# An audio tower on one core: scores in a three-buffer PSUM ring of their own, all other jobs in two single banks, v times W0 per token tile

## What is computed

```python
h = _L0_tok_ref(x, ...)    # signs of x and kernel, width-3 convolution, batch norm: (4, 748, 64)
h = h + _L0_attn_ref(_layernorm(h), Wqkv, bqkv, W0, b0)
h = h + _L0_ffn_ref(_layernorm(h), w1s, b1s, w2s, b2s)

# attention, 8 heads of 64
q, k, v = jnp.reshape(x @ Wqkv + bqkv, (3, b, n, d, h))
score = jnp.einsum('bnqh,btqh->bnth', q, k) * d ** (-0.5)
attn = jax.nn.softmax(score, axis=1)
av = jnp.einsum('bnnh,bnqh->bnqh', attn, v)      # only the diagonal of attn is used
out = av.reshape(b, n, d * h) @ W0 + b0
# feed-forward: a binary tree of 255 nodes; each token follows one path of 8 nodes,
# out = sum over the path of gelu(|logit|) * (x @ w2s[node] + b2s[node])
```

## Time and profile before

| | |
|---|---|
| median of 3 runs | 580.06 us |
| profiled execution | 581.13 us, span 579.4 us |
| TensorE matmul busy | 403.5 us, 70% |
| VectorE busy | 372.9 us, 64% |
| ScalarE busy | 277.9 us, 48% |
| GpSimd busy | 307.8 us, 53% |
| mean granted TensorE clock | 0.849 |

### The profile page before, as it was taken

One profiled execution on the slowest core, in us unless ns is written; L12 is line 12 of the kernel. 1 busy time (PEld: TensorE's weight loads), 2 busy tenths in 40 slices (PEclk: granted clock), 3 DMA queues, 4 the chain that ended last, 5 costly groups with the idle time before them and its releaser, 6 DMA issues.

```text
span 579.4 us, 8416 instructions
## 1 busy us (share of the span) xinstructions
PE 403.5 (70%) x2782; PEld 286.3 (49%) x2782; DVE 372.9 (64%) x605; ACT 277.9 (48%) x615; POOL 307.8 (53%) x354
## 2 busy tenths in 40 slices
PE   1335688887987898888858898622314999287781
PEld 1224566565655565556645665411213777154550
DVE  0756757668677667774678586872982999733431
ACT  1344578768667866776637577410201010044541
POOL 2665308563355177843456771398746677752211
PEclk9977789989889987988869789955555999689997
DMA  4251404319969123212303120084004110200000
GB/s 115 70 120 47 115 13 107 92 42 215 193 127 158 36 67 79 59 37 66 81 0 80 37 72 1 7 124 75 12 12 126 31 41 24 76 9 4 5 6 10
DMA packets 57822, 37.53 MB, mean 65 GB/s; under 512 B 30846, under 2 KB 56429, under 8 KB 57772
## 3 DMA queue, kind: packets, MB, share of 16 engines
q1 hardware_dynamic: 54030, 33.96, 26.7%
q0 software_dynamic: 2944, 2.45, 1.5%
q10 hardware_dynamic: 800, 0.49, 0.3%
HBM read 11.33 MB, written 9.56 MB: 36 GB/s over the span
## 4 chain that ended last, share of the span: by engine, by line
PE 41%; DVE 24%; ACT 16%; issue 8%; POOL 7%; DMA 3%; ACTq 0%; SPq 0%; DVEq 0%; POOLq 0%
PE Z L834 11%; ACT Z L1099 7%; PE Z L963 4%; PE Z L790 4%; DVE lm L1456 4%; PE Z L746 4%; PE Z L737 4%; PE Z L792 3%; DVE nm L1258 3%; DVE va L1449 3%; ACT k L1043 3%; ACT q L1043 2%; PE Z L965 2%; DVE va L1284 2%; PE Z L815 2%
## 5 line engine op out<-in xcount | busy, mean ns | idle before, releaser
L1258 DVE TENSOR_REDUCE nm<-Z 125x1 f32<-125x748 f32 x192 | 172.8, 931 | 94.4 <-PE Z L834 91.8
L1099 ACT ACTIVATE Z<-Z,nm 125x748 f32<-125x748 f32 x192 | 164.9, 860 | 74.8 <-DVE nm L1258 74.6
L834 PE MATMUL Z<-pool_a 128*125 128x512 f16 (+1 forms) x768 | 162.7, 357 | 18.9 <-ACT Z L1099 12.6
L834 PEld LDWEIGHTS Z<-pool_a 128*125 128x125 f16 x768 | 98.6, 151 | 62.3 <-ACT Z L1099 20.9
L667 POOL DMA_INDIRECT out<-lm,va x44 | 43.1, 979 | 59.4 <-DVE lm L1462 52.7
L545 POOL TENSOR_TENSOR pool_a<-q,pool_a 128x748 f16<-128x748 f32 x16 | 26.2, 1635 | 60.4 <-DVE pool_a L1221 60.3
L1456 DVE TENSOR_REDUCE lm<-va 128x64 f32<-128x512 f32 x44 | 45.2, 1027 | 1.3
L790 PE MATMUL Z<-va,xhT 128*125 128x128 f16 x192 | 33.1, 257 | 17.4 <-ACT Z L1099 17.4
L1178 ACT COPY va<-Z 32x512 f32<-32x512 f32 x48 | 27.5, 573 | 34.5 <-PE Z L969 34.5
L1099 ACT ACTIVATION_READ_ACCUMULATOR Z<-Z,nm 125x1 f32 x192 | 39.5, 206 | 0.0
L737 PE MATMUL Z<-xhT,wq 128*128 128x249 f16 (+2 forms) x256 | 33.1, 278 | 8.7 <-ACT Z L1099 7.6
(11 more groups left out here) (208 smaller groups left out, 690.1 us busy)
## 6 DMA issues: line engine op xcount, KB each, us to landing
pool_a<-pool_a SPq DMA_DIRECT2D x64, 187.0 KB, 3.3
pool_a<-pool_a SPq DMA_DIRECT2D x64, 93.5 KB, 2.2
sorted_rows<-zrow SPq DMA_DIRECT2D x1, 3864.0 KB, 22.7
va<-sorted_rows SPq DMA_DIRECT2D x11, 276.0 KB, 5.4
w<-in_L_ffn_w2s SPq DMA_DIRECT2D x1, 2048.0 KB
lm<-in_x SPq DMA_DIRECT2D x4, 375.0 KB
pool_a<-in_L_ffn_w2s SPq DMA_DIRECT2D x1, 1024.0 KB
out<-lm,va POOLq DMA_INDIRECT x44, 2.2
```

The source lines that it names most:

```text
L834: last = mm(z[0:XP, c0:c1], kst[:, u % 3, a, hd, KST[t]:KST[t] + XP], qst[:, u % 3, hd, c0:c1], start=(a == 0), stop=(a == 1))
L1099: sc_.activation(z, z, ACT.Exp, bias=nm[0:XP, u % 4, i:i + 1], accum_out=sm[0:XP, u % 4, i:i + 1]).then_inc(s_fa, 1)
L1258: v.tensor_reduce(nm[0:XP, u % 4, i:i + 1], zone(("s", u, i))[0:XP, 0:N], X, ALU.max, negate=True).then_inc(s_max, 1)
```

## The change

1. **PSUM.** Scores alone go round three double buffers, `Z[n % 3]`, and wait for the exponentials three steps before. All other jobs go round two single banks, `E`, the halves of `Z[3]`, and wait for the job two before. Jobs are cut to fit 512 columns: q and k in two parts each, the transposes and ranks in two, the logits in three, the diagonal in three pieces behind three steps.
2. **v times W0.** For batches 0 to 2 a job is now one token tile for all eight heads (`yt`, three matmuls of 512 columns), six a batch, in the first two units after it (`ph` 0 and 1). `weigh_heads` handles 512 columns; `add_heads` halves them by three additions on GpSimd and adds the result to h. Batch 3 keeps pairs of heads (`yp`), in two parts.
3. **Tree.** GpSimd's `path_masks` goes from `ph` 3 to the next batch's `ph` 0, `leaf_masks` from 0 to 1, the layer norm from 1 to 2, `own_slots` from 0 to 3; TensorE's transposes and logits from `ph` 2 to 3 (last batch 2 to 1), ranks from 3 to 2.
4. **First stage.** x of batch 1 waits for batch 0, ScalarE's half of Wqkv is issued later; the low parts of the weights and of the first q and k go from GpSimd to VectorE (`first_lo`); `xh 1` and `normalise(2)` go behind the first scores.

```diff
-        FIRST = [("q", 0), ("k", 0), ("q", 1), ("k", 1), ("xb", 2), ("xb", 3), ("xh", 1), ("cv", 2)]
+        LASTB = NU - NPAIR
+        FIRST = [("xb", 2), ("xb", 3), ("cv", 2)]
...
             f = []
-            if 1 <= u <= NU and i == 0:
-                f.append(("d", u - 1))
-            if u + AHEAD < NU and i in (1, 3):
-                f.append(("qk"[i // 2], u + AHEAD))
-            f += {(0, 4): [("xh", 2)], (0, 5): [("cv", 3)], (0, 7): [("wt", 0)], (0, 9): [("wm", 0)],
-                  (0, 11): [("wt", 1)], (1, 2): [("wm", 1)], (1, 4): [("xh", 3)], (1, 5): [("wt", 2)],
-                  (1, 7): [("wm", 2)], (1, 9): [("cb", 0)], (1, 11): [("w1", 0)], (2, 5): [("y", 0)],
-                  (2, 9): [("y", 1)]}.get((u, i), [])
-            if 3 <= u <= NU and i == 5:
-                f.append(("y", u - 1))
-            if b >= 0 and ph == 2:
-                f += {5: [("t", b)], 8: [("l", b, 0)], 10: [("l", b, 1)]}.get(i, [])
-            if b >= 1 and (ph == 3 if b < B - 1 else ph == 1) and i == 7:
-                f.append(("r", b - 1))
-            if b == B - 1 and ph == 3 and i == 11:
-                f.append(("r", b))
+            if 1 <= u <= NU and i < 3:
+                f.append(("d", u - 1, i))
+            if u + AHEAD < NU and 3 <= i <= 6:
+                f.append(("q" if i < 5 else "k", u + AHEAD, 2 - i % 2))
+            f += {(0, 1): [("xh", 1)], (0, 2): [("wt", 0)], (0, 7): [("wm", 0)], (0, 8): [("xh", 2)], (0, 9): [("cv", 3)],
+                  (0, 11): [("wt", 1)], (1, 7): [("wm", 1)], (1, 8): [("xh", 3)], (1, 9): [("wt", 2)],
+                  (1, 11): [("wm", 2)], (2, 7): [("cb", 0)], (2, 9): [("w1", 0)]}.get((u, i), [])
+            if 0 <= b < B - 1 and ph < 2 and i in (7, 9, 11):
+                f.append(("yt", b, 3 * ph + (i - 7) // 2))
+            if u == NU - 2 and i in (7, 8, 10, 11):
+                f.append(("yp", LASTB + i // 10, (0, 1)[i in (8, 11)]))
+            if NU - 1 <= u <= NU and i in (7, 9):
+                f.append(("yp", u - 1, (i - 7) // 2))
+            if 0 <= b < B - 1 and ph == 3:
+                f += {7: [("t", b, 0)], 8: [("t", b, 1)], 9: [("l", b, 0)], 10: [("l", b, 1)], 11: [("l", b, 2)]}.get(i, [])
+            if 1 <= b and ph == 2 and i in (7, 9):
+                f.append(("r", b - 1, (i - 7) // 2))
+            if b == B - 1 and ph == 1:
+                f += {7: [("t", b, 0)], 8: [("t", b, 1)], 9: [("l", b, 0)], 10: [("l", b, 1)], 11: [("l", b, 2)]}.get(i, [])
+            if b == B - 1 and ph == 3 and i in (7, 9):
+                f.append(("r", b, (i - 7) // 2))
...
         def zone(f):
-            return Z[(number[f] + 3) % 4]
+            return E[number[f] % 2]
...
             load_x(0)
+            sp.wait_ge(s_xin[0], 16)
             load_x(1)
...
-            def w_lo(g):
...
             x_lo(0)
-            w_lo(1)
+            rstd1(1)
...
+            def add_heads(b, t):
+                k = NT * b + t
+                pool.wait_ge(s_wyv, k + 1)
+                if t == 0:
                     pool.wait_ge(s_hb, b + 1)
-                hv = xrow[0:XP, b * NT:(b + 1) * NT, C_H:C_ID]
-                pw = prod[0:XP, w % 2]
+                hv = xrow[0:XP, k, C_H:C_ID]
+                pw = prod[0:XP, k % 2, 0:8 * D]
+                for n in (4 * D, 2 * D, D):
+                    link(gp.tensor_tensor(pw[:, 0:n], pw[:, 0:n], pw[:, n:2 * n], ALU.add))
+                gp.tensor_tensor(hv, hv, pw[:, 0:D], ALU.add).then_inc(s_hy, 1)
+
...
-            part_lo("q", 0)
-            part_lo("k", 0)
             part_lo("q", 1)
             part_lo("k", 1)
-            rstd1(1)
...
                     token_numbers()
-                if u == 2:
+                if u == 3:
                     h_bias(0)
                     h_bias(1)
                     h_bias(2)
                     h_bias(3)
-                    add_heads(0)
-                    add_heads(1)
-                if 3 <= u < NU:
-                    add_heads(u - 1)
-                if 0 <= b < B - 1 and ph == 3:
-                    path_masks(b, pool, gp, link)
-                if 1 <= b and ph == 0:
-                    leaf_masks(b - 1, pool, gp, link)
-                if b >= 2 and ph == 0:
-                    own_slots(b - 2)
-                if 0 <= b < B - 1 and ph == 1:
+                if 0 <= b < B - 1 and ph < 2:
+                    for t in range(3 * ph, 3 * ph + 3):
+                        add_heads(b, t)
+                if u == NU - 2:
+                    add_pair(LASTB)
+                if NU - 2 <= u < NU:
+                    add_pair(u - 1)
+                if 0 <= b < B - 1 and ph == 2:
                     ln2_squares(b)
                     ln2_rstd(b)
                     ln2_x(b)
-                if b == B - 1 and ph == 1:
-                    ln2_rstd(b)
+                if 1 <= b and ph == 0:
+                    path_masks(b - 1, pool, gp, link)
+                if 1 <= b and ph == 1:
+                    leaf_masks(b - 1, pool, gp, link)
+                if b >= 2 and ph == 3:
+                    own_slots(b - 2)
+                if u == NU:
+                    ln2_rstd(B - 1)
                     pool.sem_inc(s_rs2, 1)
-            pool.wait_ge(*full(("s", NU - 1, 2 * NT - 1)))
+            pool.wait_ge(s_score, 2 * NT * NU)
             link(gp.memset(wlow[D:P, :], 0.0))
...
             def take(f):
-                if number[f] >= 4:
-                    pe.wait_ge(*freed[order[number[f] - 4]])
+                if number[f] >= 2:
+                    pe.wait_ge(*freed[order[number[f] - 2]])
...
+            def heads_out(b, t):
...
+                r0, g = v_tile(b, t)
+                for a in range(2):
+                    mm(z[0:XP, :], xhT[:, r0:r0 + XP], mw[:, a, g * H * D:(g + 1) * H * D], start=(a == 0), stop=False)
+                mm(z[0:XP, :], pick[:, g, 0:XP], cb[:], start=False, stop=True).then_inc(s_full, 1)
...
             def scores(u, i):
                 hd, t = divmod(i, NT)
-                z = take(("s", u, i))
+                n = 2 * NT * u + i
+                z = Z[n % 3]
+                if n >= 3:
+                    pe.wait_ge(s_exp, n - 2)
+                else:
+                    pe.wait_ge(s_first, n + 2)
...
+            def first_lo(kind):
+                n = "qk".index(kind)
+                dve.wait_ge((s_qc, s_kc)[n], 1)
+                v.tensor_tensor(hl[:, 0, n, 1, 0:N], (q32, k32)[n][:, 0, 0:N], hl[:, 0, n, 0, 0:N],
+                                ALU.subtract).then_inc(s_lo, 1)
...
             center(1, Z[1][:, 512:1024])
+            hi_cast("q", 0)
+            first_lo("q")
+            hi_cast("k", 0)
+            first_lo("k")
+            normalise(1)
             signs(2)
             signs(3)
-            hi_cast("q", 0)
-            hi_cast("k", 0)
             hi_cast("q", 1)
             hi_cast("k", 1)
-            normalise(1)
             center(2, zone(("cv", 2)))
-            normalise(2)
...
+            def weigh_heads(b, t):
+
+                k = NT * b + t
+                dve.wait_ge(s_at, NPAIR * (b + 1))
+                dve.wait_ge(*full(("yt", b, t)))
+                if k >= 2:
+                    dve.wait_ge(s_hy, k - 1)
+                w0 = NPAIR * b % 8
+                av = at[0:XP, w0:w0 + NPAIR, :].rearrange("p j (a t) -> p t j a", a=2)[:, t].unsqueeze(3).to_broadcast(
+                    [XP, NPAIR, 2, D])
+                v.tensor_tensor(prod[0:XP, k % 2, 0:8 * D].rearrange("p (j a o) -> p j a o", j=NPAIR, a=2),
+                                zone(("yt", b, t))[0:XP].rearrange("p (j a o) -> p j a o", j=NPAIR, a=2),
+                                av, ALU.mult).then_inc(s_wyv, 1)
+                dve.wait_ge(s_wyv, k + 1)
+                dve.sem_inc(s_fd, 1)
...
                         take(f)
-                    if (u, i) == (1, 1):
-                        normalise(3)
-                    if (u, i) == (1, 11):
+                    if (u, i) in ((0, 2), (1, 3)):
+                        normalise(2 + u)
+                    if (u, i) == (2, 9):
                         dve.wait_ge(s_ch, 1)
                         v.tensor_tensor(c32[:, 1, :], c32[:, 0, :], cb[0:3, :], ALU.subtract).then_inc(s_cl, 1)
-                    if 1 <= u <= NU and i == 4:
+                    if 1 <= u <= NU and i == 5:
                         diag_weights(u - 1)
-                    if u + AHEAD < NU and i in (3, 5):
-                        hi_cast("qk"[i // 4], u + AHEAD)
-                    if u == NU and i == 6:
+                    if u + AHEAD < NU and i in (6, 9):
+                        hi_cast("qk"[i // 9], u + AHEAD)
+                    if 0 <= b < B - 1 and ph == 2 and i == 2:
+                        ln2_sums(b)
+                    if 0 <= b < B - 1 and ph == 3 and i == 0:
+                        ln2_sumsq(b)
+                    if u == NU and i == 10:
                         last_heads(NU - 1)
```

(8 more changed lines are left out.)

284 lines of the change are left out of this document (150 added, 134 removed).

## The result

The changed kernel takes 584.66 us (median of 20 runs, 580.88 to 587.65); the kernel before took 583.49 in the 20 runs beside it. The ratio is 1.008, 95% interval [1.005, 1.011]: 0.8% slower, within the 2% that the prediction calls no change, but not the 570 us of the prediction. It is taken without the slow executions, over 1.5% above the fastest of their kernel, of which the kernel before had 8 and the changed kernel none; that is why it is larger than the 0.2% between the two medians. The profiled execution took 582.8 us, its span is 581.1 us at a clock of 0.823 (before: 579.4 and 0.849).

What follows compares the result with a forecast made beforehand. No engine was full in attention; engines waited for each other through the ring of four, where every other job takes a turn. 579.4 - 10 - 13 + 12 = 568.4 us of span, plus 1.7 around it: 570, range 548 to 592.

Steps and rivals of the forecast that it cites:

- the first stage: Up to the first maximum: batch 2's normalising goes behind the scores, low parts leave GpSimd; -10 us, from 3.7 to 13.
- attention: First maximum to last exponential: 315.5 us against 328.6, so -13, bounds -24 and +15.
- the tail: Behind the last exponential: GpSimd has more left and its memset may hold VectorE; +12 us, bounds +6 and +16.
- batch 2: Units 12 to 15: same wait for masks, y product parts and a wait for squares on top; 86.5 us against 82.1.
- the 6 us set apart for the clock: Over the four attention stretches: allowance for plain units at a granted clock of 0.75, 2.7 us longer each; 6 us.
- Prices of single operations: Product of 512 columns 0.70 us, a tile's additions 1.9, GpSimd's list from the cast of k to leaf masks 37.4.
- Batches 0 and 1: Units 4 to 7: 70 us against 75.7; units 8 to 11: 81 against 86.0, about 10 lost ahead of ranks.
- the last term, 19 us for unit 15: Last unit of batch 2, in the sum 52 + 15.5 + 19 = 86.5 us.
- The third: Gain drowns in GpSimd: additions take 3 us a tile or casts meet GpSimd instructions; +17, 587 us; chance 0.10.
- The second: TensorE's clock: more units at a mean clock of 0.75, attention stretches below 0.80; 594 us; chance 0.13.
- The first: Shorter units show in full: no clock loss, attention 306.5 us, first stage gives 12; 553 us; chance 0.27.
- the rule: GpSimd and VectorE's shared port pair is locked for the whole instruction; end +14 us by it, +6 without.

Runs made afterwards that it cites:

- the last kernel: Against the combined kernel: triple product buffer, VectorE's sums over h at step 8 instead of 2, ranks of batch 0 at steps 10 and 11; 550.0 us, 0.947.
- the new unit 14: Changed kernel with unit 14's y products at steps 3, 4, 7, 8 and ranks at 10, 11: 572.5 us; with sum of squares at step 3 too: 569.7.
- The run with the slots ahead of the memset: Changed kernel with the slots of batch B-2 issued on GpSimd just ahead of the large memset instead of behind it; 580.6 us, ratio 0.999.
- the combined kernel: Changed kernel with the new unit 14, sum of squares at step 3, x at once, slots of batches 0 and 1 in unit 15; 562.6 us, 0.967.
- the one with the triple buffer: Changed kernel with only the buffer of the products v times W0 made triple, so GpSimd may lag two tiles; 583.5 us, ratio 1.002.
- The last two kernels: The combined kernel with triple product buffer and sums at step 8: 557.8 us, 0.964; then also ranks of batch 0 at steps 10 and 11: 550.0, 0.947.

## Why the prediction was wrong

The forecast missed the profiled span by 12.7 us (568.4 against 581.1), and the sum shows where: +5.3 in the first stage, +10.0 in attention, -2.6 in the tail. In attention batch 2 is off by 11.4 us and the other three stretches by 4.7 together, less the 6 us set apart for the clock.

- **Prices of single operations: right.** The product of 512 columns took 0.68 us (0.70), a tile's additions 1.99 (1.9), the list to the leaf masks 38.2 (37.4). TensorE had the masks 50.6 us behind the first exponential of batch 1 (51) and 50.8 behind that of batch 2 (326.2 less 275.4; 52).
- **Batches 0 and 1: right**, 72.5 and 81.5 us against 70 and 81, although the 6 us for the clock were kept apart there. But the reason given for batch 1, "All scores stand behind it: about 10 us are lost" ahead of the ranks, was only part: TensorE waited 1.55 us there, since the waits for products and sums had held it up already.
- **Batch 2: the step that failed, in its last unit.** Up to the end of unit 14 the forecast has 52 + 15.5 = 67.5 us, and units 12 to 14 took 67.5; the wait for the squares is in it at 4 and was 4.22. What failed is the last term, 19 us for unit 15: it took 29.4. The four parts of y products were priced in unit 14 only. Unit 15 has two more, and its clock was put at nothing there. By the terms that the forecast names (12.5 + 3 + 17 + 4) the sum would also be 2 us larger than the 15.5 + 19 that it carries.

The last five steps of a unit with transposes and logits, from the exponential of step 7: unit 11 of the changed kernel, unit 15 of it, and unit 15 of the last kernel, with the same jobs on TensorE as the second (the counts differ by what else falls into the window):

```profile
268.10:275.40 7.30, 6.39 (x39) 4.96 (x37) 4.93 (x6) 6.66 (x16) 4.15 (x3) 1.00 0.53 126
357.50:372.20 14.70, 11.60 (x44) 8.48 (x42) 4.67 (x6) 6.64 (x15) 4.85 (x5) 0.64 0.04 12
```

```profile
337.30:348.30 11.00, 7.90 (x50) 6.17 (x48) 4.76 (x7) 6.62 (x15) 6.79 (x8) 1.00 0.11 34
```

At a clock of 1.00 the two y parts, which take turns in the two banks with the transposes and logits, cost 3.7 us; in both kernels TensorE waits 1.68 and 1.42 us there for a bank that VectorE empties. The same jobs at 0.64 take 3.7 more. With the 3.8 us by which the first seven steps are longer than those of unit 11, mostly the wait for the squares, that gives 29.4 from the 18.2 of unit 11. No run moves the two y parts of unit 15, so their price is read from these rows and not from an experiment. The 10.7 us that the new unit 14 took back are no miss of the forecast: they are waits that it had priced, and that another order avoids.

- **First stage: mis-sized.** I let the normalising of batch 2 go behind the scores and counted -10; it gave -4.7. The centring of batch 2 stayed ahead, with three operations at 1.47 to 2.07 us beside GpSimd (0.56 alone), and x of batch 1 came 2 us later. With both put right the first exponential stood at 41.6 us instead of 47.7. Besides, the term is not worth its size: the 3.2 us that the centring won at the first exponential came back in unit 0.
- **Tail: right**, +9.4 of +12 with bounds of +6 and +16, and VectorE's step was held. The run with the slots ahead of the memset shows what moving it is worth, 3.8 us, with another step then held for 3.49.
- **Rivals.** The third, at 587, came nearest in time, not in mechanism: the additions took what they should, and no cast of q or k took more than 0.80 us. The second spoke of a clock under 0.80; that came in batch 2 alone (0.77), and rose to 0.84 there (274.3 to 361.5 us of that run) when the jobs were reordered. So it holds in part, in batch 2, where unit 15 alone shows 3.7 us of it. The first is refuted as a forecast, but the last kernel, at 550.0, shows that the gain was there.

## What to carry to other kernels

When a slow engine's list has several readers, find all of them before moving one: each looks cheap in the trace (1.5 us for the masks, 1.3 for the sums), because the one in front hides the next, and the whole only shows when the last is moved. When a ring is made smaller, price a job not only by its length but by when its bank is emptied, in every unit that has the job, and look at what is queued on the emptying engine between. A wait of the critical engine costs nothing by itself while the engine behind it is still busy. Where a step is to be hidden in idle time of the critical engine's neighbour, check that the start that it wins isn't paid for in the next unit.

## What was not expected of the hardware

**Which VectorE steps a memset on GpSimd holds.** In the combined kernel the memset began before the ranks, and reductions ran beside it at their usual length (0.95 us for 768 columns); only the TENSOR_SCALAR was held to its end:

```profile
381.84 8.73 POOL L670 MEMSET pool_a<- 64x10368 f32 x1 [0.15 <-POOL run L338]
...
386.78 0.95 DVE L1387 TENSOR_REDUCE rank<-gt 128x6 f32<-128x768 f32 x1
...
389.84 0.78 DVE L1433 TENSOR_SCALAR lgb<-lg 128x42 f32<-128x42 f32 x1
```

In the first stage it was the operations with two operands in SBUF (L1250, L1254, L1255) that grew beside GpSimd's low parts and products, and not the reduction between them (L1252, 0.55 us, beside L522). The Trainium skill (SBUF — State Buffer, section "Who interferes with whom") makes just these distinctions: steps with one SBUF input are free outside the two-port modes, those with two meet a GpSimd instruction that reads, and copies, casts and scalar steps take the pair in the two-port modes. The traces agree. My prediction had used the rule as if it held for every VectorE instruction. It had +14 by the rule and +6 without it; the tail grew by 9.4.

**The same stretch at different clocks.** Units 1 and 2 are alike in the changed kernel and in the one with the triple buffer (the first and second row), and yet:

```profile
69.80:107.40 37.60, 32.59 (x205) 23.53 (x206) 26.67 (x38) 31.57 (x75) 19.71 (x34) 0.89 0.29 67
```

```profile
69.20:111.00 41.80, 37.20 (x205) 27.87 (x206) 26.98 (x38) 31.98 (x74) 19.71 (x34) 0.76 0.26 60
```

These are 4.2 us at a granted clock of 0.76 instead of 0.89, and only TensorE's matmuls and weight loads are busy for longer (by 4.6 and 4.3 us); the other engines differ by 0.4 us at most. In the profiled executions of the 19 changed kernels these two units took from 35.8 to 42.9 us. The last two kernels show what that does to a total: their profiled executions differ by 0.6 us, though the second is 5.9 us shorter in the three batches, since its units 0 to 3 took 77.9 us instead of 72.3. What sets the clock of this stretch in an execution is not shown. Small edits are therefore better read from the stretch they touch than from the total.
